# Order of the first transfers in a cross-attention and feed-forward kernel: a signal of its own for the layer norm's scales, value weights and second pair of tiles first, query and key scales on SP

## The reference

```
xn = layernorm(x, ln_x_g, ln_x_b)        # x here: the context
ln = layernorm(latents, ln_l_g, ln_l_b)  # latents: _layernorm(block input)
q = ln @ W_q
kv = concatenate([xn @ W_kv, ln @ W_kv]);  k, v = halves of kv, 4 heads of 64
qn = rmsnorm(q, q_gamma) * SCALE;  kn = rmsnorm(k, k_gamma)
sim = qn . kn, masked;  attn = softmax(sim);  out = (attn @ v) @ W_out + b_out
x = x + out
x = x + ffn(_layernorm(x))               # ternary weights, 8-bit activations, conv of width 3
```

## Time and profile before

| what | us |
|---|---|
| median of 3 runs | 479.63 |
| lowest and highest | 477.93, 480.08 |
| the profiled execution, its own time | 480.25 |
| span of its trace | 478.2 |
| PE busy | 415.0 (87%) |
| DVE busy | 391.1 (82%) |
| ACT busy | 313.0 (65%) |

### The profile page before, as it was taken

How to read it: one execution, slowest core, us unless ns; L and a number is a source line. 1 busy time by engine, 2 the same in 40 slices (tenths; PEclk the granted TensorE clock), 3 DMA queues, 4 the chain that set the end, 5 groups by cost and what they waited for, 6 DMA issues and landing times.

```text
span 478.2 us, 15103 instructions
## 1 busy us (share of the span) xinstructions
PE 415.0 (87%) x5910; PEld 282.9 (59%) x5910; DVE 391.1 (82%) x635; ACT 313.0 (65%) x359; POOL 78.3 (16%) x93
## 2 busy tenths in 40 slices
PE   0999985489999999999699899899899977798876
PEld 0666664146666666666476566666576644565664
DVE  4389999299978789879669878889878899999964
ACT  1356675156697766666556656656756567889866
POOL 2075554560000111010102002002001010000000
PEclk9999999599999999999999999999999995999989
DMA  8700000521211211111111111111111000010001
GB/s 231 183 1 1 1 2 10 179 94 45 67 46 35 68 35 45 58 35 45 48 36 45 56 36 45 58 34 45 41 33 42 1 0 2 0 45 23 24 24 66
DMA packets 27447, 22.56 MB, mean 47 GB/s; under 512 B 7229, under 2 KB 26878, under 8 KB 27390
## 3 DMA queue, kind: packets, MB, share of 16 engines
q1 hardware_dynamic: 25978, 21.72, 14.2%
q10 hardware_dynamic: 1412, 0.01, 0.2%
HBM read 7.04 MB, written 2.10 MB: 19 GB/s over the span
## 4 chain that ended last, share of the span: by engine, by line
PE 49%; DVE 21%; issue 14%; ACT 13%; ACTq 2%; DMA 1%; DVEq 1%
PE sc L1355 13%; DVE arena L698 7%; PE heads L1372 6%; PE heads L1373 5%; PE heads L1374 5%; ACT arena L1083 4%; PE heads L1251 3%; PE sc L1260 2%; PE by L1408 2%; ACT qq L1166 2%; ACT qq L1158 1%; DVE arena L592 1%; PE by L1528 1%; PE sc L1511 1%; PE heads L1511 1%
## 5 line engine op out<-in xcount | busy, mean ns | idle before, releaser
L698 DVE SCALAR_TENSOR_TENSOR arena<-arena 128x1024 bf16<-128x1024 f32 x160 | 196.2, 1260 | 40.3 <-ACT arena L1083 39.9
L1083 ACT ACTIVATE arena<-sc,kb 128x1024 f32<-128x1024 f32 x160 | 170.2, 1113 | 90.0 <-PE sc L1355 89.8
L1372 PEld LDWEIGHTS heads<-v,arena 128*128 128x128 bf16 x1280 | 117.7, 97 | 47.2 <-issue 34.2
L1372 PE MATMUL heads<-v,arena 128*128 (+1 forms) x1280 | 131.0, 194 | 10.3 <-DVE arena L698 8.9
L1355 PE MATMUL sc<-qs,kst 64*128 64x512 f16 x960 | 121.0, 385 | 11.7 <-issue 9.9
L1373 PE MATMUL heads<-v,arena 128*128 (+1 forms) x1280 | 129.6, 195 | 0.0
L1374 PE MATMUL heads<-v,arena 128*128 (+1 forms) x1280 | 129.0, 193 | 0.0
L1374 PEld LDWEIGHTS heads<-v,arena 128*128 128x128 bf16 x1280 | 119.1, 99 | 0.0
L1373 PEld LDWEIGHTS heads<-v,arena 128*128 128x128 bf16 x1280 | 118.9, 98 | 0.3
L1355 PEld LDWEIGHTS sc<-qs,kst 64*128 64x128 f16 x960 | 42.7, 95 | 59.2 <-issue 21.0
L470 POOL TENSOR_SCALAR frs<-fmv 128x2 f32<-128x2 f32 x8 | 7.0, 869 | 165.4 <-DVE fmv L750 165.4
(11 more groups left out here) (185 smaller groups left out, 590.5 us busy)
## 6 DMA issues: line engine op xcount, KB each, us to landing
kst<-kk SPq DMA_DIRECT2D x80, 128.0 KB, 2.0
xs<-in_x SPq DMA_DIRECT2D x8, 256.0 KB, 6.7
qs<-qq SPq DMA_DIRECT2D x16, 128.0 KB, 2.3
out<-cbuf SPq DMA_DIRECT2D x7, 256.0 KB, 2.1
xs<-in_ctx SPq DMA_DIRECT2D x6, 256.0 KB, 7.3
xs<-in_L_ffn_w SPq DMA_DIRECT2D x1, 1024.0 KB, 5.5
cbuf<-in_L_ffn_w SPq DMA_DIRECT2D x1, 1024.0 KB, 9.1
arena<-in_L_xattn_W_kv SPq DMA_DIRECT2D x1, 512.0 KB, 6.3
```

The lines of the kernel that those rows point to most:

```text
L698: e.scalar_tensor_tensor(out=rest[:, j, :, :], in0=prob[:, j, :, :], scalar=SHRINK, in1=probh[:, j, :, :], op0=ALU.mult, op1=ALU.subtract) ...
L1083: a_.activation(prob[:, j, :, :], sc[j % 2][:, :, :], ACT.Exp, bias=kb[:, bass.ds(i * QUAD + j, 1)]).then_inc(exp_done[j], 1)
L1372: t_.matmul(o, hi, row[:, 0:OW], start=first and sub == 0, stop=False, skip_group_check=True)
```

## The change

SP: the transfer of `W_kv` is cut into its value half and its key half. SP's order becomes pair 0, value weights, pair 1, key weights, `W_q`, pairs 2 to 7, the six pairs of context, then the six transfers of query and key scales that ACT issued before, and the rest as it was. The value weights count up a semaphore of their own, `w_values`; key and query weights count up `w_proj`.

ACT: issues four transfers (the layer norm's scales and biases), which count up a new semaphore `ln_in`, and waits for that one alone.

PE: the wait for `w_proj` moves from its very start to the first `project`; the first `project_values` waits for `w_values`.

DVE: `gamma_product` waits for the six transfers of `w_norm` and moves from turn -3 to the end of turn -1.

```diff
         def _(sp):
             sp.dma_start(xs[:, 0:2, :], xt[:, 0:2, :]).then_inc(d_x[0], 16)
+            sp.dma_start(wqkv[:, :, 2 * INNER:3 * INNER], w_kv[:, INNER:2 * INNER].rearrange("(k p) n -> p k n", p=P)).then_inc(s["w_values"], 16)
+            sp.dma_start(xs[:, 2:4, :], xt[:, 2:4, :]).then_inc(d_x[1], 16)
+            sp.dma_start(wqkv[:, :, INNER:2 * INNER], w_kv[:, 0:INNER].rearrange("(k p) n -> p k n", p=P)).then_inc(s["w_proj"], 16)
             sp.dma_start(wqkv[:, :, 0:INNER], w_q.rearrange("(k p) n -> p k n", p=P)).then_inc(s["w_proj"], 16)
-            sp.dma_start(wqkv[:, :, INNER:3 * INNER], w_kv.rearrange("(k p) n -> p k n", p=P)).then_inc(s["w_proj"], 16)
-            for n in range(1, XP):
+            for n in range(2, XP):
...
+                for i in range(2):
+                    sp.dma_start(gq[i * DH:(i + 1) * DH, 0:1], q_gamma.rearrange("(d a) -> d a", a=1)).then_inc(s["w_norm"], 16)
+                    sp.dma_start(gq[i * DH:(i + 1) * DH, 1:2], k_gamma.rearrange("(d a) -> d a", a=1)).then_inc(s["w_norm"], 16)
+            sp.dma_start(grow[64:65, 0:DH], q_gamma.rearrange("(a d) -> a d", a=1)).then_inc(s["w_norm"], 16)
+            sp.dma_start(grow[64:65, DH:2 * DH], k_gamma.rearrange("(a d) -> a d", a=1)).then_inc(s["w_norm"], 16)
             sp.wait_ge(s["zero_ready"], 1)
...
             def gamma_product():
-                dve.wait_ge(s["w_norm"], 16 * 10)
+                dve.wait_ge(s["w_norm"], 16 * 6)
...
-                if isinstance(i, int) and i == -3:
+                if isinstance(i, int) and i == -1:
                     gamma_product()
...
-            act.wait_ge(s["w_norm"], 16 * 10)
+            act.wait_ge(s["ln_in"], 16 * 4)
...
             pe.wait_ge(s["consts"], 6)
-            pe.wait_ge(s["w_proj"], 32)
...
             def project_values(n, par):
                 wait(pe, "lnt_ready", n + 1)
+                if isinstance(n, int) and n == 0:
+                    pe.wait_ge(s["w_values"], 16)
...
             def project(n, kind, par):
+                if isinstance(n, int) and n == 0:
+                    pe.wait_ge(s["w_proj"], 32)
```

More of the change, by code:

```diff
@@ L219, in xattn_ffn @@
         probh = arena[:, 0:QUAD * 2 * CHUNK].bitcast(BF16).rearrange("p (k e c two) -> p k e c two", k=QUAD, e=2, two=2)[:, :, :, :, 1]
-        names = """w_norm w_rest w_proj mask_in w_ffn pairs_in ident_ready consts zero_ready count_step
+        names = """ln_in w_norm w_rest w_values w_proj mask_in w_ffn pairs_in ident_ready consts zero_ready count_step
             count_ready scale_ready limit_ready max_ps max_step max_taken qst_ready kq_ready shift_col shift_ps
@@ L343, in _ @@
                              crow[r0:r0 + 2 * P, :].rearrange("(t p) d -> p t d", p=P)).then_inc(d_c[n], 16)
+            with nc.allow_non_contiguous_dma(reason="a few hundred numbers, one per partition"):
+                for i in range(2):
[3 more added lines that the diff above has]
+            sp.dma_start(grow[64:65, DH:2 * DH], k_gamma.rearrange("(a d) -> a d", a=1)).then_inc(s["w_norm"], 16)
             sp.wait_ge(s["zero_ready"], 1)
@@ L997, in _ @@
                 for i, (gain, bias) in enumerate(((ln_l_g, ln_l_b), (ln_x_g, ln_x_b))):
[L998 to L1004, removed]
+                    act.dma_start(lng[:, i, :, 0], gain.rearrange("(k p) -> p k", p=P)).then_inc(s["ln_in"], 16)
+                    act.dma_start(lng[:, i, :, 1], bias.rearrange("(k p) -> p k", p=P)).then_inc(s["ln_in"], 16)
             act.wait_ge(s["consts"], 1)
             a_.activation(largest_score[:, 0:1], halves[:, 0:1], ACT.Exp)
-            act.wait_ge(s["w_norm"], 16 * 10)
+            act.wait_ge(s["ln_in"], 16 * 4)
             def evacuate(n, g0, par):
```

## The result

| | before | after |
|---|---|---|
| median, us (11 runs each) | 479.3 | 481.75 |
| lowest and highest | 477.72, 480.1 | 481.14, 485.08 |
| profiled execution: own time, span | 480.25, 478.2 | 483.31, 481.4 |

The ratio of after to before is 1.0065, 95% interval 1.0046 to 1.0083: slower by 3.1 us (2.2 to 4.0), where 3.2 was forecast (482.8 against a median of 479.63). The two medians lie 2.45 us apart. The front works as meant and the time is lost behind it, on the path that was named. The execution that was profiled after the change is the second slowest of the eleven, so what its trace shows is more than the change costs on average; the terms are compared further down over several traces.

What follows compares the result with a forecast made beforehand. PE, busy 87% of the span, was taken to bound the kernel, with DVE at 82%. A later start of 0.7 plus 2.4 us of clock gave +3.1 on 480.25, 483.4, or 482.8 us against the median; range 478.8 to 486.5.

Steps and rivals of the forecast that it cites:

- The front: Kernel start: `gains(0)` at 8.9 instead of 12.07, `project_values(0)` at 10.0 instead of 13.14, 3.1 us earlier.
- the path that was named: First 30 us: SP's issues and count of `pairs_in`, to DVE's `stats(3)`, then `v_low(1)`, then PE's `project_values(2)`.
- Bound and path: First 30 us: the chain runs through ACT's ten transfers to PE; the path behind `pairs_in` has only 0.47 us of slack.
- SP's list: SP's issues before `pairs_in`: new ones cost 2.3 us, half hidden, so `pairs_in` 1.2 us later and `project_values(2)` 0.7 us later.
- half of what two long issues could hide: SP's `cb` and `bout`: excesses of 0.96 and 1.66 us might hide the 2.3 us; half taken, 1.2 us.
- The clock: PE's new 3.8 us idle before `project_values(2)`: granted clock falls to 0.50, costing 2.4 us, bounds 0 and 3.1.
- two other idle times: PE late in the kernel: idle times of 3.91 and 2.08 us both brought the granted clock from 1.00 to 0.50.
- what was to be seen: Profile after: PE idle 3 to 5 us before the third `project_values`, granted clock 0.5 behind it for 3 to 6 us.
- a clock that holds: PE's gap too short for the clock; with SP's issues hidden, 479.2 to 480.2 us; chance of hidden 0.28.
- `gamma_product`: DVE: five instructions, 1.0 us, move behind `normed(3)`; idle time takes 0.8, the rest meets 1.3 us of room: nothing.
- The sum: Whole kernel: 0.7 us later start plus 2.4 us clock, +3.1 us, 482.8 us against the median.
- The rule that spoke against it: SP's issuing: by the Trainium skill's rule, moving the scales to SP costs nothing; the forecast disagreed, since SP's sequencer is waited for.

Runs made afterwards that it cites:

- e3: The changed kernel with the six transfers of query and key scales issued by ACT again, behind its four: 480.07 us, ratio to the kernel before 1.002.
- e4: The changed kernel with five more matrix products on PE ahead of `project_values(2)`, filling its idle time: 482.52 us, ratio to the kernel before 1.0064.
- e6: The changed kernel with five small products at PE's very start, where it idles anyway: 483.78 us, ratio to the kernel before 1.0106.
- e9: The kernel before with five small products at PE's very start, where it idles anyway: 480.43 us, ratio to the unmodified kernel before 1.0032.
- e1: The changed kernel with `stats(3)` to `stats(7)` waiting for their own pair's transfer instead of `pairs_in`: 476.45 us, ratio to the kernel before 0.9938.
- e2: The kernel before with `stats(3)` to `stats(7)` waiting for their own pair's transfer: 478.36 us, ratio to the unmodified kernel before 0.9989.
- e5: The changed kernel with `stats(3)` to `stats(7)` waiting for their own pair and ACT issuing the six scales: 476.5 us, ratio to the kernel before 0.9948.
- e11: e6 once more, beside e10 on the same chip: 484.5 us, ratio to the kernel before 1.0097.
- e8: The kernel before with e2's direct waits, `ln_in` for ACT's first four transfers and `gamma_product` at turn -1, weights as before: 477.0 us, ratio 0.996.
- e10: e4 once more, beside e11 on the same chip: 482.51 us, ratio to the kernel before 1.0079.

## Why the prediction was right

**Bound and path.** Right, and shown. The small slack behind `pairs_in` decided the case. It was 0.40 us rather than 0.47: in e3, e4, e6, e9 and the changed kernel PE's waiting `project_values(2)` starts 0.83 us after `v_low(1)` starts, which gives 26.92 before. e1 removes this wait alone and the kernel is faster than before; e2 bounds what it cost in the kernel before at 1.2 us, with 0.5 as the middle value. e9 and e2 show how thin the cover was: with PE 0.7 us early in e9's trace, `project_values(2)` waited 0.43 us for `v_low(1)` in the kernel before as well.

```profile
26.76 1.97 PE L1253 MATMUL heads<-arena 128*128 128x256 f32 x8 [0.43 <-DVE v L584]
```

**The front.** Forecast 3.1 us, measured 2.56 in the changed kernel's trace and 3.1 in the traces of e1, e3, e4 and e5. Its scales had landed by 9.5, for 8.9 forecast. As said, it made no difference to the end.

**SP's list.** I took 1.2 us, half of what two long issues could hide. Measured: 2.23 us later at `stats(3)` (25.87 for 23.64). Of it 1.3 us are the list itself, from its own end points, and e4 (12.4 us for the same stretch) and e3 (11.0) confirm it. The other 0.9 us are the pace of the transfers before the list, which I had taken as fixed: the last context issue ended at 12.4 here, and at 11.2 and 11.8 in e4 and e1, whose lists are the same. Where that stretch was faster `stats(3)` came at 24.77 (e4), 24.80 (e11) and 25.12 (e6), so the forecast of 24.8 fits some executions and not the one profiled. The halving was nearly right for the wrong unit prices: the six issues cost 3.9 us, not 2.6, and more of them was hidden, 2.5 us behind the mask, `cb` and `bout`.

**The clock.** It fell, as forecast from two other idle times. I took 2.4 us; the trace has 3.0, those of e3, e6 and e11 1.8, 2.7 and 1.5, and the runs 1.5 on average with a wide error. The idle time, 5.10 us, and the low stretch, 6.8 us, lie just outside what was to be seen (3 to 5 and 3 to 6). An idle time of about 4 us does not always bring the clock down before PE resumes: in e3, after 3.98 us, it fell 0.1 us behind PE's start, and late in the kernel, after 3.91 us, it fell 1.3 us ahead of PE's start in the kernel before, but in e5 and e8 only some 5 us behind it, when PE had worked and idled for another 2.8 us. The forecast had a clock that holds only as its lower bound.

**`gamma_product`.** Forecast at nothing. In e1, where it would show, PE has no idle time at all in the first 60 us beyond its first two waits: right.

**The sum.** 0.7 + 2.4 = 3.1 us was forecast. The trace of the stage has 1.82 + 3.04 = 4.86, so both terms were too small there, the first by more than half, and that the two profiled spans still differ by 3.2 only comes from the 1.6 us of their tail, which the sum did not have. Over the three traces that have this list and this stall the terms are 1.82, 1.08 and 0.75 us for the start and 3.0, 2.7 and 1.5 for the clock (changed kernel, e6, e11): 1.2 and 2.4 on average, 3.6 in all. So the clock's term was well sized and the start's too small by half a microsecond. The mechanism was right. That the number met the measured 3.1 to a tenth is luck: one trace and the next differ by more than 2 us in these two terms, the interval of the runs is 1.8 us wide, and products that nobody needs moved the time by 1.5 us (e9).

**The rule that spoke against it.** The Trainium skill, "DMA: Bandwidth & Descriptors", section "Issuing engines are not separate DMA queues", calls the sequencer's time "usually small relative to the DMA itself". For one transfer that holds here too: 0.23 to 1.09 us to issue a scale on SP, where one of them took 4.76 us from issue to landing on ACT. But six of them took 3.9 us in a row, and DVE waited for a signal that SP gives behind its whole list. e3 is the comparison: with the six on ACT `stats(3)` starts at 24.05, with them on SP at 25.87. In this kernel the move was not free.

## What to carry to other kernels

A signal that an issuing engine gives by its own instruction is only as early as the whole list in front of it. Before adding transfers to such an engine, look for waits on what stands behind them, and let consumers wait for the transfer's own semaphore. When the head of a pipeline is made faster, check the next path behind it first: a gain of 3 us met only 0.4 us of slack, and an idle time of PE costs more than its length when the clock falls in it. An experiment that adds instructions to an engine needs a control that adds as many in a harmless place.

## What was not expected of the hardware

Five products of 128x128 at PE's start, in idle time, made the kernel before slower by 0.32% (0.14 to 0.5) and the changed one by 0.3 to 0.4% (e6 and e11 against its 1.0065). The traces show where one part may lie: PE's idle time of no shown releaser near 236 us was 4.89, 4.9 and 5.1 us in e4, e10 and e11, but 3.5 in e6 and 3.3 in e9, against 3.4 to 3.7 in the seven kernels without added instructions. So it is longer in three of five executions, and not in all; where the time went in e6 and e9, and whether it is the length of the stream or something else about these products that matters, stays open. It also means that any difference here of 1 to 2 us between two kernels can hold a part that has nothing to do with their idea; the gain of the earlier front together with the direct waits does not rest on one such pair, since three different kernels (e1, e5, e8) show it, 1.9 to 3.0 us by their ratios.

The same six transfers of scales took between 0.24 and 1.22 us each to issue on ACT and between 0.23 and 1.09 on SP. A price for issuing read from one place of a trace is no unit price for another.
